# Rotary attention's weighted sum in three fp32r passes, and table work ahead of the routing

## What is computed

```python
x = x + tanh(g_xattn[0]) * windowed_attention(layernorm(x), ctx)      # 8 heads, window 16
x = x + tanh(g_ffn[0])   * lora_ffn(layernorm(x))                     # base matmul + top-2 of 8 rank-16 experts
x = x + tanh(g_xattn[1]) * rotary_attention(layernorm(x), ctx, ctx)   # 32 query heads, 8 key-value heads of 128
x = x + tanh(g_ffn[1])   * gptq_ffn(layernorm(x))                     # 4-bit weights, silu(x Wg) * (x Wu), Wd

# rotary_attention, for each batch of 64 rows and each head:
attn = softmax(rope(q) @ rope(k).T / sqrt(128) + mask)
out = attn @ v            # then out @ wo
# lora_ffn: router logits, top 2, weights w; out = x @ W_base.T + b + sum_e w_e * (x A_e) B_e * 2
# gptq_ffn unpacks w4 = (qweight >> shift) & 15, W = (w4 - (z4 + 1)) * scale
```

## Time and profile before

| what | us |
|---|---|
| median of 3 runs | 1049.38 (1047.78 to 1050.95) |
| the profiled execution | 1050.37, its span 1048.6 |
| TensorE busy | 1001.5 (96%) |
| TensorE weight fetches | 723.6 (69%) |
| VectorE busy | 683.5 (65%) |
| GpSimd busy | 548.6 (52%) |
| ScalarE busy | 438.9 (42%) |

### The profile page before, as it was taken

The page is one execution under the profiler, slowest core; times in us unless marked ns, Lnnn a source line. Parts: engine busy times, 40 slices in busy tenths (PEclk is TensorE's granted clock), DMA queues, the critical chain, the costliest instruction groups (busy, mean ns, idle before and its releaser), DMA issues. The chain is left out here.

```text
span 1048.6 us, 13770 instructions
## 1 busy us (share of the span) xinstructions
PE 1001.5 (96%) x4712; PEld 723.6 (69%) x4712; DVE 683.5 (65%) x1079; ACT 438.9 (42%) x1263; POOL 548.6 (52%) x392
## 2 busy tenths in 40 slices
PE   5899999898799999999999999999999989999998
PEld 2444444455577777778777777777778767888787
DVE  7999999847876767666667677765556553322223
ACT  4344443341245555454455465544544532221131
POOL 5676777644677666676577677752341211222021
PEclk9899999998999999999999999999999999999999
DMA  8000000012215433342344354310120005110002
GB/s 288 1 1 1 1 1 1 0 43 79 69 62 162 126 97 109 120 142 92 102 132 131 123 178 156 118 54 26 51 61 1 1 1 180 49 41 16 1 1 80
DMA packets 60532, 75.93 MB, mean 72 GB/s; under 512 B 8012, under 2 KB 43636, under 8 KB 60456
## 3 DMA queue, kind: packets, MB, share of 16 engines
q1 hardware_dynamic: 56176, 57.75, 17.3%
q0 software_dynamic: 4144, 17.04, 5.4%
q10 hardware_dynamic: 144, 0.27, 0.1%
HBM read 64.37 MB, written 10.68 MB: 72 GB/s over the span
## 5 line engine op out<-in xcount | busy, mean ns | idle before, releaser
L859 PE MATMUL ps<-xh,wqh 128*128 128x512 f32 (+1 forms) x432 | 175.3, 406 | 1.7 <-DVE xl L851 1.4
L861 PE MATMUL ps<-xh,wql 128*128 128x512 f32 (+1 forms) x432 | 169.3, 392 | 0.0
L860 PE MATMUL ps<-xl,wqh 128*128 128x512 f32 (+1 forms) x432 | 168.3, 390 | 0.0
L1551 POOL TENSOR_TENSOR shared<-shared 128x512 f32<-128x512 f32 x64 | 87.1, 1361 | 136.4 <-DVE shared L1712 135.7
L1627 ACT ACTIVATE c_xn<-c_xn,c_mn 128x64 f32<-128x64 f32 x256 | 85.9, 337 | 90.4 <-DVE c_mn L1726 90.4
L859 PE MATMUL ps<-woh,oh 128*128 128x512 f32 x256 | 103.4, 404 | 4.3 <-DVE ol L1738 4.3
L1710 DVE TENSOR_TENSOR shared<-ps,cs 128x512 f32<-128x512 f32 x80 | 55.2, 690 | 72.0 <-PE ps L861 70.1
L860 PE MATMUL ps<-wol,oh 128*128 128x512 f32 x256 | 101.5, 396 | 0.0
L861 PE MATMUL ps<-woh,ol 128*128 128x512 f32 x256 | 101.3, 396 | 0.0
L859 PEld LDWEIGHTS ps<-xh,wqh 128*128 128x128 f32 (+1 forms) x432 | 80.7, 187 | 26.7 <-issue 10.0
L422 POOL TENSOR_TENSOR r<-r 128x1024 f32<-128x1024 f32 x32 | 76.3, 2383 | 40.1 <-DVE r L661 39.2
(11 more groups left out here) (187 smaller groups left out, 2158.1 us busy)
## 6 DMA issues: line engine op xcount, KB each, us to landing
stage<-in_wq SPq DMA_DIRECT2D x16, 512.0 KB
stage<-in_wo SPq DMA_DIRECT2D x16, 512.0 KB
w_wide<-dq SPq DMA_DIRECT2D x32, 172.0 KB, 2.7
stage<-w_wide SPq DMA_DIRECT2D x20, 256.0 KB, 3.1
qraw<-in_gate_qweight SPq DMA_DIRECT2D x16, 172.0 KB
qraw<-in_up_qweight SPq DMA_DIRECT2D x16, 172.0 KB
qraw<-in_down_qweight SPq DMA_DIRECT2D x10, 256.0 KB
w_down<-dq SPq DMA_DIRECT2D x10, 256.0 KB, 2.4
```

Source lines behind the costliest of these rows:

```text
L859: pe.matmul(dst, lh, rh, start=(first and c == 0), stop=False)
L860: pe.matmul(dst, lh, rl, start=False, stop=False)
L861: last = pe.matmul(dst, ll, rh, start=False, stop=(final and c == chunks - 1))
L1551: pool.tensor_tensor(qT[:, h * TPH:(h + 1) * TPH, :, p - 1, :], turn(ra), turn(rb), ALU.add)\
```

## The change

- **Weighted sum.** v and the turned probabilities are split: vh and ah are ScalarE's copies (fp32r), vl and al new subtracts on VectorE (`low_values` once a slot, `low_turned` once a step). `weighted` makes three passes (vh ah, vh al, vl ah) over both halves, six fp32r matmuls instead of two fp32 ones. It waits for `al_ready`, and so does the next `turn`.
- **Hold.** GpSimd waits in each step with a unit for VectorE's unpack of the next unit before it does the low piece and the rest of the step.
- **Low-rank stage.** The zeros of down, the tables and `row_indices` come ahead of the wait for the logits. Rows are normalised on ScalarE (Identity with scale and bias), and VectorE computes only the bias (`shift`).
- **Gate and up.** `norm_turn` of tile EARLY + 2 comes one product earlier.
- Memory: lah and lal end early, s lies where aT lay, the row buffer of the rotary stage is dq.

```diff
+            with ExitStack() as early:
+                for name in ("lah", "lal"):
+                    g[name] = sbuf(early, name, [P, DC, NE * RANK + NE], F32R)
+            for name in ("vh", "vl"):
+                g[name] = sbuf(first, name, [P, NT, DK], F32R)
...
+                          ("s", 2 * (GRP // 2) * BT * C))
...
@@ -1050,6 +1053,7 @@
...
+        shift = sb("b_shift", [P, NT])
...
@@ -1208,9 +1213,19 @@
...
-            for i in range(LORA_ROWS):
-                act.wait_ge(out_done, i + 1)
-                norm_high(act, g, n2, XT2, i)
+            def rows_normalised(i):
+                act.wait_ge(shift_ready, i + 1)
+                if i >= 2:
+                    act.wait_ge(n2["xt_done"], i - 1)
+                act.activation(xn[:, i % 2, :], x[:, i, :], ACT.Identity, scale=g["rstd"][:, i:i + 1],
+                               bias=shift[:, i:i + 1]).then_inc(n2["xn_ready"], 1)
+
+            for i in range(LORA_ROWS + 1):
+                if i < LORA_ROWS:
+                    rows_normalised(i)
+                if i >= 1:
+                    act.wait_ge(out_done, i)
+                    norm_high(act, g, n2, XT2, i - 1)
...
@@ -1224,6 +1239,9 @@
...
             unpack_zeros(dve, g, slice(0, 2 * GK), INTER)
+            link(unpack_zeros(dve, g, slice(DOWN_ROW, DOWN_ROW + GD), D))
+            tables_of_zeros(dve, g)
+            row_indices(dve, g, link)
             dve.wait_ge(lg_done, 1)
...
@@ -1271,19 +1289,17 @@
...
-            link(unpack_zeros(dve, g, slice(DOWN_ROW, DOWN_ROW + GD), D))
-            tables_of_zeros(dve, g)
             weighted_hidden(0)
             for i in range(NT):
                 add(i)
                 if 0 <= i - 1 < LORA_ROWS:
                     dve.wait_ge(rstd_ready, i)
-                    norm_rows(dve, g, n2, xn, i - 1)
+                    dve.scalar_tensor_tensor(shift[:, i - 1:i], g["mv"][:, i - 1, 0:1], -1.0, g["rstd"][:, i - 1:i],
+                                             ALU.mult, ALU.mult).then_inc(shift_ready, 1)
                 if 0 <= i - 3 < LORA_ROWS:
                     norm_low(dve, g, n2, XT2, i - 3)
                 if i == 1:
                     weighted_hidden(1)
-                    row_indices(dve, g, link)
             norm_low(dve, g, n2, XT2, LORA_ROWS - 1)
...
@@ -1425,18 +1441,19 @@
...
-        v = sb("v", [P, NT, DK])
+        vh, vl = g["vh"], g["vl"]
...
-        xn = sb("c_xn", [P, 2, D])
-        s, pr = (xn[:, j, :].rearrange("p (b k) -> p b k", b=2) for j in range(2))
+        s = g["s"]
+        pr = sb("pr", [P, 2, KEYS])
...
-        aT = g["aT"]
+        ah = sb("ah", [P, 2, KEYS], F32R)
+        al = sb("al", [P, 2, KEYS], F32R)
...
+        xn, xn3 = g["dq"], g["sz"][:, :, 0:D]
...
@@ -1557,10 +1575,12 @@
...
                 due = piece_due(c, last)
+                u = unit_at(step_number(b, c))
+                if u is not None and u + 1 < Q_UNITS:
+                    pool.wait_ge(g["qn_ready"], u + 2)
                 if due:
                     piece, db, odd = due
                     low_piece(pool, g, b + db, odd, piece)
-                u = unit_at(step_number(b, c))
                 if u is not None:
                     subtract_zeros(pool, g, u)
                     multiply_scales(pool, g, u)
...
-                act.activation(v[:, h * TPH:(h + 1) * TPH, :],
+                act.activation(vh[:, h * TPH:(h + 1) * TPH, :],
                                ps[:, value_banks(b, sl)[1], :].rearrange("p (i d) -> p i d", i=TPH),
-                               ACT.Copy).then_inc(v_ready, 1)
+                               ACT.Copy).then_inc(v_high, 1)
...
-                act.activation(aT[:, c % 2, :], ps[:, TR, 0:KEYS], ACT.Copy).then_inc(aT_ready, 1)
+                act.activation(ah[:, c % 2, :], ps[:, TR, 0:KEYS], ACT.Copy).then_inc(ah_ready, 1)
...
+            def low_values(b, sl):
+                h = sl % NHALF
+                tiles = slice(h * TPH, (h + 1) * TPH)
+                dve.wait_ge(v_high, SLOTS2 * b + sl + 1)
+                dve.tensor_tensor(vl[:, tiles, :], ps[:, value_banks(b, sl)[1], :].rearrange("p (i d) -> p i d", i=TPH),
+                                  vh[:, tiles, :].bitcast(F32), ALU.subtract).then_inc(v_ready, 1)
+
+            def low_turned(b, c):
+                dve.wait_ge(ah_ready, step_number(b, c) + 1)
+                dve.tensor_tensor(al[:, c % 2, :], ps[:, TR, 0:KEYS], ah[:, c % 2, :].bitcast(F32), ALU.subtract)\
+                   .then_inc(al_ready, 1)
...
                 if tile_exists(c, last):
                     minimum(b, c)
+                if tile_exists(c - 2, last):
+                    low_turned(b, c - 2)
...
                     low_out(b, c - 2)
                 if tile_exists(c, last):
                     one_over_sums(b, c)
+                if projecting(c, last) and j == 3:
+                    low_values(b, sl + 1)
                 for p in units[1]:
...
             rotary(0, 0, 1)
+            low_values(0, 0)
             norm_low(dve, g, n, XT, LORA_ROWS)
...
                 m = step_number(b, c)
                 pe.wait_ge(pr_ready, m + 1)
                 if c >= 1:
-                    pe.wait_ge(aT_ready, m)
+                    pe.wait_ge(al_ready, m)
...
             def weighted(b, c):
 
                 m, i = step_number(b, c), c % NT
-                pe.wait_ge(aT_ready, m + 1)
+                pe.wait_ge(al_ready, m + 1)
                 if c >= 1:
                     pe.wait_ge(ol_ready, m)
                 if c % TPH == 0:
                     pe.wait_ge(v_ready, SLOTS2 * b + c // TPH + 1)
-                for k in range(BT):
-                    rows = slice(k * C, (k + 1) * C)
-                    last = pe.matmul(ps[:, PV[k], 0:KEYS], v[rows, i, :], aT[rows, c % 2, :], start=True, stop=True)
+                for n_pass, (values, weights) in enumerate(((vh, ah), (vh, al), (vl, ah))):
+                    for k in range(BT):
+                        rows = slice(k * C, (k + 1) * C)
+                        last = pe.matmul(ps[:, PV[k], 0:KEYS], values[rows, i, :], weights[rows, c % 2, :],
+                                         start=(n_pass == 0), stop=(n_pass == 2))
                 last.then_inc(pv_done, 1)
...
-            pe.wait_ge(aT_ready, STEPS2 * PAIRS)
+            pe.wait_ge(al_ready, STEPS2 * PAIRS)
...
@@ -2106,8 +2145,8 @@
             norm_turn(pe, g, n, xn, XT, EARLY)
             gate_up_products(pe, g, 1, 0, 0)
             norm_turn(pe, g, n, xn, XT, EARLY + 1)
+            norm_turn(pe, g, n, xn, XT, EARLY + 2)
             gate_up_products(pe, g, 1, 0, 1)
-            norm_turn(pe, g, n, xn, XT, EARLY + 2)
             pe.wait_ge(n["xl_ready"], NT)
             for t, hf in GU_ORDER[2:]:
                 products(t, hf)
```

More of the change, by code:

```diff
@@ L135, in build_program @@
         with ExitStack() as first:
-            for name in ("lah", "lal"):
-                g[name] = sbuf(first, name, [P, DC, NE * RANK + NE], F32R)
+            with ExitStack() as early:
[3 more added lines that the diff above has]
+                g[name] = sbuf(first, name, [P, NT, DK], F32R)
             g["index"] = sbuf(first, "index", [P, Q_UNITS], U32)
@@ L1082, in routed_lora @@
         rstd_ready = sem("rstd_ready")
+        shift_ready = sem("shift_ready")
         c_landed = [sem(f"c_landed{i}") for i in range(C_RING)]
@@ L1456, in rotary_attention @@
         vtr_done = sem("vtr_done")
+        v_high = sem("v_high")
         v_ready = sem("v_ready")
@@ L1464, in rotary_attention @@
         aT_done = sem("aT_done")
-        aT_ready = sem("aT_ready")
+        ah_ready, al_ready = sem("ah_ready"), sem("al_ready")
         pv_done = sem("pv_done")
```

4 lines of the change are left out of this document (1 added, 3 removed).

## The result

The changed kernel takes 1034.97 us (median of 4 runs, 1033.69 to 1038.42), the kernel before in the same comparison 1048.64: a ratio of 0.9867, 95% interval 0.9839 to 0.9895, 13.7 us less by the medians. Forecast were 1037.5 us and a range of 1033 to 1046.

A forecast was written before the change was run, and what follows sets the result against it. The prediction took TensorE, busy 96% of the span, as the bound, with waits to win outside the main rotary part. Its terms, -3.9 - 1.2 - 5.3 - 1.5 = -11.9 us off the median 1049.38, gave 1037.5 us, range 1033 to 1046.

The forecast's parts named there:

- Weighted sum: Rotary stage: three fp32r passes replace two fp32 pairs, 0.067 us less in each of 58 steps, -3.9 us (-5.8 to -2.3).
- The first rival: Weighted sum: weight fetches not hidden in half-array passes, each pass 0.21 us, +12.5 us, run at 1053.9; chance 0.10.
- the rule quoted from the Trainium skill: Weighted sum: a weight fetch overlaps running matmuls only when its row group differs; the basis of a slower rival.
- The new wait: Rotary stage: TensorE's weighted sum waits for al from VectorE, about 0.46 us after ScalarE's copy; forecast hidden, costing nothing.
- The hold, and the stalls: Rotary stage: GpSimd's hold shortens unpacks at no cost; stalls at the stage's start and one later give -1.2 us (0 to -1.5).
- the fourth rival: Rotary stage: hold fails, unpacks stay long, al is 1.2 us late in seven short steps, run at 1045.9; chance 0.07.
- Low-rank stage: Low-rank stage: earlier tables and ScalarE norms remove TensorE waits, -4.3 us and -1.0 us, together -5.3 us (-2.5 to -7.5).
- late next: Low-rank stage: GpSimd's scales, then ScalarE's rows behind the last context chunk (near 252.7, used at 253.8), become late next.
- The third rival: Low-rank stage: tables delay routing, GpSimd is the bound, the stage gains only 1 us, run at 1041.8; chance 0.13.
- the range's best bounds: Whole kernel: all terms at their best bounds sum to -16.3 us, giving the range's fast end of 1033 us.
- The last steps: Last six rotary steps: TensorE waits for VectorE anyway, the new subtract fits by 0.1 us, cost taken as 0.
- Gate and up: Gate and up: moving the last row tile's norm_turn ahead of 12 matmuls removes TensorE's xl wait, -1.5 us (-1.0 to -1.7).

The follow-up runs named there:

- exchanged loops: Changed kernel with the weighted sum's loops swapped, three passes of one array half and then those of the other: 1036.57 us, ratio 0.9875 to the kernel before.
- fp32 sum: Changed kernel with the weighted sum again one fp32 product for each half, no low halves, hold kept: 1037.62 us, ratio 0.9879 to the kernel before.
- zeros twice: Changed kernel with VectorE's unpack of the down zeros done a second time ahead of the routing: 1035.38 us, ratio 0.9871 to the kernel before.
- old turn: Changed kernel with gate and up's last norm_turn back behind the first column of products: 1038.30 us, ratio 0.9888 to the kernel before.
- norms on VectorE: Changed kernel with low-rank rows normalised on VectorE again, tables still ahead of the routing: 1036.74 us, ratio 0.9868 to the kernel before.
- index arithmetic back: Changed kernel with only the index arithmetic back behind the second half of the hidden products: 1036.97 us, ratio 0.9878 to the kernel before.

## Why the prediction was right, point by point

**Weighted sum** (-3.9): right in mechanism and size. The taking apart of a pair into 0.11 of fetch, 0.11 of stream and 0.1 of emptying came out as 0.22, 0.12 and 0.55 in all; measured is 0.077 a step for 0.067, and -3.8 with the start of the stage. The first rival (a pass of 0.21) is dead: behind the first, exposed fetch the passes are 0.12 apart. With it goes the rule quoted from the Trainium skill, "TensorE: Matmul & The Clock Gate", section "The mechanism": the fetch at 594.78 runs beside the products of its own rows, and with the loops exchanged 0.09 us in 55 steps are lost, so the trace does not agree with it. The same section also names fetches into the background weight buffer as ones that are pulled ahead, and with that the trace can agree; my prediction left it out. The new wait was to cost nothing; that held in all steps but the first, where it was 0.55.

**The hold, and the stalls** (-1.2): right in kind, too small in size. The main part gave -0.61. Steps 0 to 3 gave -1.43 net; in fp32 they are 22.75 for 24.57 before, -1.82. Together -2.4, for a forecast -1.2 and a bound of -1.5. What I had priced as the fourth rival, al late by 1.2 us in seven short steps (8.4 us), is what the run without the hold shows: 1.20 to 1.34 in six and 2.44 in one, and 2.6 at the start, of which 1.5 are a slow clock. The unpack was to take 0.40 under the hold and takes 1.11 in the step shown and 1.54 at most, since the rotary sum is still running beside it; al was 1.1 us ahead of need as forecast. The hold itself cost nothing: TensorE waits nowhere for wql or wkvl.

**Low-rank stage** (-5.3, measured -7.5, at the far bound): the term that was mis-sized. Three of its steps held: one gap of 3.27 us for a forecast 3.5, the logits at 235.4 for "near 236", norms cheap on ScalarE (0.82 for 0.6). TensorE's own work from the first hwT product on came to 24.5 us for a forecast 24. Up to the stage's end TensorE stood 9.84 us before (4.60 in 240 to 253, 5.24 after) and 4.88 in the changed kernel (0.53, 2.75 and 1.60): 5.0 less, near the 5.3. The step that failed is "it will run slowly for a while after this gap as it did after the old one, no change". 7.9 less at the end, 5.0 of waits and 0.4 from the start leave 2.5. About 2.0 of it can be read directly as the slow stretch: from the first hwT product to the next of its kind TensorE does the same work in 7.18 us before (247.72 to 254.90) and in 5.20 in the changed kernel (246.05 to 251.25). The stretch was gone in the profiled execution; in the two runs with the stage (nearly) unchanged that had one (exchanged loops, zeros twice) it ended before 248 and took the place of a wait. So the clock in this stage differs from run to run, but the gain does not hang on it: with the fall the stage was 58.27, without it 58.21. Who is the bound came out as forecast: I had GpSimd 4 us ahead of TensorE, from 26 us of work, and most waits gone. GpSimd's last work of the stage ends at 270.47 (27.3 us from 243.17 on, 2.0 of them waits for VectorE's sums), and TensorE, which waits for nothing from 254.50 on, ends the stage 1.4 us later; the one wait left, 1.37 us for the first row (254.50), is at the place that I had named as late next, with ScalarE's rows. The third rival, in which GpSimd is the bound and costs the gain, did not come. In the range's best bounds I mis-added: they give -16.5 and not -16.3, which moves nothing.

**The last steps** (0): 27.40 for 27.42. The new subtract fits ahead of the add (VectorE):

```profile
823.57 0.43 DVE L1758 TENSOR_TENSOR al<-ps,ah 128x256 fp32r<-128x256 f32 x1 [1.18 <-ACT ah L1665]
824.25 0.75 DVE L1784 SCALAR_TENSOR_TENSOR x<-ps,gate,x 128x512 f32<-128x512 f32 x1 [0.25 <-PE ps L864]
```

**Gate and up** (-1.5): -1.68, and 1.76 when undone.

That the total came near is no cancelling of errors: each of the four terms has its sign and its mechanism, and the two that were off, the stalls and the low-rank stage, were both too small.

The parts measured one by one (3.8, 7.5, 1.7, and 12.7 for the hold) add up to far more than 15.9, since the hold and the passes are not independent: in fp32 the hold is worth at most the 2.4 above, with the passes 12.7 (10.04 + 2.63, with the 1.5 of a slow clock). My sum treated them as one and was right for that reason; read as separate gains it would have called the passes a gain alone, and alone they are a loss.

## What to carry to other kernels

Before an exact split puts a new small operation on a helper engine's queue between producer and TensorE, look at what stands ahead of it in that queue in the shortest step: here a gain of 4 us was a loss of 5 or more as long as an unpack could stand ahead of it for over 4 us. Work that one engine shares with GpSimd is cheapest where GpSimd is idle, however early that is, and some small operations suffer most in proportion. When a wait goes, size separately what the clock did behind it, and check whether a slow clock falls into time in which TensorE would have waited anyway.

## What the runs showed of the hardware

- The two halves of the array ran side by side whichever half's products came first in the program (486.11 against 486.02 us for 55 steps), with records still in pairs; the halves' products then did not start in the program's order.
- Some VectorE operations of a few columns took about as long as the GpSimd operation running beside them: 0.15 us became 2.30 (shift, beside the 2.35 piece), 0.18 became 1.24, 0.28 became 1.38. Others did not: the one below ran while GpSimd did a low piece from 248.11 to 249.40, and the subtract, mask and reduce operations of 128x256 at 414.4 to 416.2 stayed at 0.42 beside a piece. Why these are spared no run here isolates.

```profile
248.84 0.15 DVE L1290 TENSOR_SCALAR veps<-mv 128x1 f32<-128x1 f32 x1
```

- The granted clock after nearly the same gap differed: 1.00 after 3.27, 3.50 (fp32 sum) and 3.52 us (no hold, old turn), 0.57 after 3.29 and 3.34, 0.50 after 3.52 (norms on VectorE). So the gap's length alone does not decide in this range; after 4.24 and more it fell in every run. Nor does a short gap keep it full: after 1.78 in this stage it stayed full, but at the start of the rotary stage it fell to 0.57 behind a wait of 1.65 in the run without the hold, and stayed full behind one of 1.66 in the run with the index arithmetic back. What else decides stays open.
